# Down's ten full blocks in seven products for eight, on one Trainium2 core

## The reference

```python
def lora_add(base, inp, A, B):
    t = einsum('bri,bni->bnr', A[0][idx], inp)           # rank 16
    return base + einsum('bor,bnr->bno', B[0][idx], t) * 0.5
gate = lora_add(x @ W_gate.T, x, A_gate, B_gate)         # F = 2752
up   = lora_add(x @ W_up.T,   x, A_up,   B_up)
act  = silu(gate) * up
x1   = x + lora_add(act @ W_down.T, act, A_down, B_down) # the part called Down
base = x1 @ weight.T + bias                              # the part called out
out  = x1 + base + scale * ((x1 @ a_sel.T) @ b_sel.T)
```

## Time and profile before

| | us |
|---|---|
| median of three runs | 1662.97 |
| the profiled execution | 1659.71 |
| its span | 1657.6 |
| TensorE busy | 1620.2 |
| VectorE busy | 1138.4 |
| GpSimd busy | 653.5 |
| ScalarE busy | 500.8 |

### The profile page before, as it was taken

One profiled execution on the slowest core, in us unless ns is written; L12 is line 12 of the kernel. 1 busy time (PEld: TensorE's weight loads), 2 busy tenths in 40 slices (PEclk: granted clock), 3 DMA queues, 4 the chain that ended last, 5 costly groups with the idle time before them and its releaser, 6 DMA issues.

```text
span 1657.6 us, 20957 instructions
## 1 busy us (share of the span) xinstructions
PE 1620.2 (98%) x7060; PEld 1315.6 (79%) x7060; DVE 1138.4 (69%) x1302; ACT 500.8 (30%) x833; POOL 653.5 (39%) x441
## 2 busy tenths in 40 slices
PE   6989999999999899999999999999999999999998
PEld 4778888888887788888888788888888887778886
DVE  5987777777769877777777655666655578856433
ACT  3633333333346333333334221111111121431110
POOL 5244444444453444454444443233323331541110
PEclk9999999999999999999999999999999999999999
DMA  8334434433533345334334751122222131013322
GB/s 160 101 80 106 151 98 105 144 84 87 131 90 101 80 108 153 92 105 143 87 85 131 249 148 58 51 79 80 80 53 78 61 70 27 19 29 79 79 50 54
DMA packets 218125, 156.12 MB, mean 94 GB/s; under 512 B 110692, under 2 KB 200164, under 8 KB 215268
## 3 DMA queue, kind: packets, MB, share of 16 engines
q1 hardware_dynamic: 169536, 114.92, 27.4%
q10 hardware_dynamic: 48356, 39.86, 7.6%
q0 software_dynamic: 128, 0.00, 0.0%
HBM read 115.38 MB, written 39.32 MB: 93 GB/s over the span
## 4 chain that ended last, share of the span: by engine, by line
PE 64%; DVE 2%; POOL 1%; issue 1%; DMA 0%; ACT 0%; SPq 0%; DVEq 0%; ACTq 0%
PE ps L1958 64%; DVE tw_down L958 0%; POOL act L1884 0%; POOL Wd L1892 0%; DVE acc L950 0%; DVE X_T L608 0%; DMA raw<-in_x_dram 0%; POOL W L1843 0%; DVE Bd L904 0%; ACT W L1397 0%; DVE Bf L641 0%; DVE tw_down L933 0%; DVE tw_down L931 0%; DVE TU L508 0%; DVE ct L1077 0%
## 5 line engine op out<-in xcount | busy, mean ns | idle before, releaser
L1958 PE MATMUL ps<-X_T,W 128*128 128x512 f32 x1944 | 463.9, 393 | 13.0 <-DVE vbuf L688 5.1
L1958 PE MATMUL ps<-act,Wd 128*128 128x512 f32 x2016 | 462.2, 389 | 1.3 <-POOL Wd L1892 1.3
L1958 PEld LDWEIGHTS ps<-X_T,W 128*128 128x128 f32 x1944 | 365.9, 189 | 97.4 <-DVE vbuf L673 7.4
L1958 PEld LDWEIGHTS ps<-act,Wd 128*128 128x128 f32 x2016 | 378.4, 188 | 81.4 <-POOL Wd L1892 1.7
L1958 PE MATMUL ps<-X_B,W 128*128 128x512 f32 x1728 | 419.0, 392 | 15.3 <-ACT X_B L1426 12.8
L1958 PEld LDWEIGHTS ps<-X_B,W 128*128 128x128 f32 x1728 | 326.4, 189 | 86.6 <-issue 13.2
L950 DVE TENSOR_TENSOR acc<-acc,ps 128x1024 f32<-128x1024 f32 x176 | 214.1, 1219 | 176.5 <-PE ps L1958 175.8
L1843 POOL TENSOR_TENSOR W<-s,W 128x512 fp32r<-128x512 f32 x156 | 211.6, 1357 | 260.4 <-ACT W L1397 260.4
L1843 POOL TENSOR_TENSOR W<-TG,W 128x512 fp32r<-128x512 f32 x88 | 128.4, 1460 | 179.3 <-ACT W L1397 179.3
L1397 ACT ACTIVATE W<-s 128x512 fp32r<-128x512 f32 x156 | 98.4, 632 | 275.5 <-PE ps L1958 264.4
L1884 POOL TENSOR_TENSOR act<-stage,act 128x1024 fp32r<-128x1024 f32 x42 | 100.7, 2415 | 173.4 <-ACT act L1630 173.4
(11 more groups left out here) (135 smaller groups left out, 1522.7 us busy)
## 6 DMA issues: line engine op xcount, KB each, us to landing
stage<-act_scratch SPq DMA_DIRECT2D x21, 1024.0 KB, 5.0
raw<-in_L_cond_W_gate_dram SPq DMA_DIRECT2D x164, 128.0 KB, 3.0
raw<-in_L_cond_W_up_dram SPq DMA_DIRECT2D x164, 128.0 KB, 3.2
raw<-in_x_dram SPq DMA_DIRECT2D x104, 128.0 KB, 3.1
raw<-in_L_cond_W_down_dram SPq DMA_DIRECT2D x88, 128.0 KB, 3.3
act_scratch<-c21buf ACTq DMA_DIRECT2D x42, 256.0 KB, 2.4
act_scratch<-vbuf ACTq DMA_DIRECT2D x42, 256.0 KB, 2.8
xt_scratch<-xt ACTq DMA_DIRECT2D x4, 2048.0 KB, 6.6
```

The lines of the kernel that those rows point to most:

```text
L1958: return nc.tensor.matmul(dst, stationary, moving, start=start, stop=stop, skip_group_check=True)
```

## The change

Down's ten full blocks are now done in seven products for eight as well, over (two halves of the output tiles, even and odd) x (the two tiles of a block) x (two groups of 512 tokens). The work is cut into 140 steps:

- The ten blocks form two groups of five (`GROUP`). In a group the products come in the order P4, P2, P1, P5, P6, P3, P7, each for both halves `h` of the tokens: 28 stages (`B_STAGES`) of five steps. A step multiplies one block's stationary part (128 x 4 x 128) by one moving block (128 x 512): 4 banks x 3 = 12 matmuls. The five steps of a stage add up in the same four banks. In P2, P1, P3 and P7 two adapter matmuls follow each step.
- Seven banks are used in turn, four to a stage (`bank_of`), and the eighth holds the adapter's sums. When a stage has ended, VectorE adds each of its banks to one to four places of `acc` (`read_bank`) during the first three steps of the next stage.
- The moving blocks are act tiles (P1, P2, P3) or sums of them (P4 to P7). The sums T1 to T4 are made by VectorE in the gate/up stage, four subtractions for each pair of full units (`t_first`, `t_second` twice, `t_fourth`), and stored to HBM (`sums_scratch`). A second `vbuf` makes room for this.
- In Down each moving block is loaded by its own DMA of 256 KB into a ring of four (`load_moving`), its high part is made by ScalarE and its low part by GpSimd (`moving_low`), for both halves of the tokens. P7 needs a second moving block, B12, for the adapter; its low part is made by VectorE.
- The weights of eight blocks at a time are held unsplit in `DW` (`turn_down`). VectorE changes them in place into the sums (`down_sum`), and the parts for one product of five blocks are split into `Sr`.
- x is added to `acc` in 16 residual items, in the middle of Down, and no longer loaded into it.
- `turn_ad(bb)` for the blocks 1 to 10 runs at the steps of `AD_STEP`; SP loads for the step `q + 4`. The turns of `Bd`, `bd_low`, `td_first` and the copies they need now run after the last step.

The core of the diff:

```diff
+        PRODUCTS = ["P4", "P2", "P1", "P5", "P6", "P3", "P7"]
+        B_GIVES = {"P1": ("C11", "C12", "C21", "C22"), "P2": ("C11",), "P3": ("C12",), "P4": ("C21",),
+                   "P5": ("C12", "C22"), "P6": ("C12", "C21", "C22"), "P7": ("C21", "C22")}
+        B_STAGES = [(g, name, h) for g in range(2) for name in PRODUCTS for h in range(2)]
+        STEPS = GROUP * len(B_STAGES)
+        def raw_at_step(q):
+            items = []
+            if 40 <= q < 88 and q % 3 == 1:
+                items.append(("r", (q - 40) // 24, (q - 40) // 3 % 8))
+            if q in (-1, 0, 1):
+                items += [("D", q + 3, 0), ("D", q + 3, 1)]
+            if 22 <= q < 34 and q % 2 == 0:
+                items.append(("D", 5 + (q - 22) // 4, (q - 22) // 2 % 2))
+            if 61 <= q < 65:
+                items.append(("D", 8 + (q - 61) // 2, (q - 61) % 2))
...
+        AD_STEP = {1: 3, 2: 5, 3: 7, 4: 9, 5: 68, 6: 70, 7: 72, 8: 74, 9: 76, 10: 100}
...
+        def mv_step(n):
+            return MOVING[n - T_RING][0] + 1 if n >= T_RING else n - 3
+        def bank_of(s, p):
+            return (4 * s + p) % 7
...
+            def t_second(U):
+                n = pairs_before(U) + 1
...
+                V.tensor_tensor(vbuf0[:, :], vbuf1[:, :], vbuf0[:, :], ALU.subtract).then_inc(t_made[2], 1)
+                eng.wait_ge(t_stored[0], 16 * n)
+                V.tensor_tensor(t1buf[:, :], vbuf1[:, :], t1buf[:, :], ALU.subtract).then_inc(t_made[1], 1)
+
+            def t_fourth(U):
+                n = pairs_before(U) + 1
+                eng.wait_ge(act_stored[0], 16 * (U + 1))
+                eng.wait_ge(t_made[1], n)
+                V.tensor_tensor(c21buf[:, :], c21buf[:, :], t1buf[:, :], ALU.subtract).then_inc(t_made[3], 1)
...
@@ VectorE, unit(U)
                 if not plain(U - 1):
                     second_act(U - 1)
+                if u % 2:
+                    t_first(U - 1)
+                else:
+                    t_second(U - 1)
                 add_q(U)
...
                 if u in SPILL_UNITS:
                     turn_x(("y", h, SPILL_UNITS.index(u)))
+                if u % 2 == 0:
+                    t_fourth(U - 1)
                 add_v(U)
...
@@ VectorE, last_unit(U)
                 else:
-                    turn_item(("D", 0, 1))
+                    turn_down(0, 1)
                     half_tile_first(U)
                     turn_ad(0)
                 half_tile_second(U)
+                if h == 1:
+                    turn_down(1, 0)
+                    turn_down(1, 1)
...
@@ VectorE, Down
+            def turn_down(bb, e):
...
+                for c in range(2):
+                    last = V.transpose(
+                        DW[bb % len(DW)][:, c, :, e * 64:(e + 1) * 64].rearrange("p k (q i) -> p q k i", q=2),
+                        src[:, :].rearrange("p (q k c i) -> p c q k i", q=2, k=KT, c=2)[:, c])
+                last.then_inc(dw_turned.up((bb, e)), 1)
...
+            def read_bank(s, p):
+                eng.wait_ge(pe_s.sem, pe_s.after(("bank", s, p)))
+                for place in places_of(s, p):
+                    h, k, c = place
+                    dst, src = acc[h][:, k, c * TT:(c + 1) * TT], bank_b(bank_of(s, p))
...
+                        V.tensor_tensor(dst, dst, src, ALU.add).then_inc(acc_added.up((s, p, place)), 1)
...
+            def down_step(q):
+                s, banks = banks_at_step(q) if q >= 0 else (0, ())
+                for p in banks:
+                    read_bank(s, p)
+                    if p == 0 and s in T_STAGES:
+                        read_t_bank(s)
+                for item in raw_at_step(q):
+                    if item[0] == "r":
+                        add_residual(item)
+                for n in range(len(MOVING)):
+                    if mv_step(n) == q and mv_by_vector(n):
+                        moving_low(n)
...
+                    if at_ < len(STILL) and STILL[at_] in sw_sum.value:
+                        down_sum(STILL[at_])
+                for item in raw_at_step(q):
+                    if item[0] == "D" and item[1] < BLOCKS - 1:
+                        turn_down(*item[1:])
+                    elif item[0] != "r":
+                        turn_item(item)
+                for bb in range(1, BLOCKS):
+                    if AD_STEP[bb] == q:
+                        turn_ad(bb)
+                if q in (STEPS - 3, STEPS - 2):
+                    last_low(q - STEPS + 3)
...
-            for bb in range(BLOCKS - 1):
-                down_block(bb)
+            for q in range(-3, STEPS + 3):
+                down_step(q)
+            for pr in range(2):
+                td_first(pr)
+            for p in range(2):
+                bd_low(p)
+            for p in range(2, 4):
+                turn_item(("Bd", p))
             last_block()
...
@@ SP
+            def load_moving(n):
+                _, name, j, h = MOVING[n]
+                if n >= STAGING:
+                    wait_mv_low(sp, n - STAGING)
...
+            def down_step(q):
+                for n, moving in enumerate(MOVING):
+                    if moving[0] == q + 6:
+                        load_moving(n)
+                for item in raw_at_step(q + 4):
...
+                for bb in range(1, BLOCKS):
+                    if AD_STEP[bb] == q + 4:
+                        load_ad(bb)
...
@@ GpSimd
+            def down_step(q):
+                for n in range(len(MOVING)):
+                    if mv_step(n) == q and not mv_by_vector(n):
+                        moving_low(n)
+                for n in {-3: (0, 1), -1: (2,), 0: (3,), 1: (4,)}.get(q, ()):
+                    still_low(STILL[n])
+                if still_for(q - 1) is not None:
+                    still_low(still_for(q - 1))
...
@@ TensorE
+            def down_step(q):
+                s, j = divmod(q, GROUP)
...
+                eng.wait_ge(sw_lo, still_at[g, name, block_] + 1)
+                wait_mv_low(eng, n)
+                for p in range(4):
+                    if j == 0 and before_in_bank[s, p] is not None:
+                        wait_bank_read(eng, *before_in_bank[s, p])
...
+                    for wl, xl in THREE:
+                        last = matmul(bank_b(bank_of(s, p)), slot[:, wl, p, :], moving[:, xl, :],
+                                      start=(j == 0 and (wl, xl) == (0, 0)),
+                                      stop=(j == GROUP - 1 and (wl, xl) == (1, 0)))
```

756 lines of the change are left out of this document (474 added, 282 removed).

## The result

The changed kernel takes **1712.7 us** (median), the kernel before 1662.2 us: a ratio of 1.031, 95% interval 1.029 to 1.032. So it is slower, as forecast, but by some 50 us where 15 were forecast. The profiled execution has a span of 1710.5 us against 1657.6 us, 52.9 us more, and that is the sum to explain. Ratios leave out slow outliers, of which there was one, 3729 us in one of the twelve executions of e12_combined_start.

What follows compares the result with a forecast made beforehand. The prediction took TensorE, busy for 98% of the span, to bound the kernel. Its terms, -54.5 + 4.9 + 6.5 + 25 + 14 + 6 + 1 + 12 = +15 us, gave 1678 us (range 1664 to 1692).

Steps and rivals of the forecast that it cites:

- around the P7 stages: Down, around the two P7 stages: a loss of 1 us.
- What is removed: Down's ten blocks: 240 fewer matmuls at 0.227 us each save 54.5 us.
- Gate/up: New VectorE subtractions cost 4.9 us in eight even spill units and 6.5 us at the heads of the halves.
- The heads: Heads of gate/up's two halves: VectorE has no idle time, so the subtractions cost 6.5 us.
- Start of Down and the adapter chain: Down's first steps: serial adapter rounds of 9.5 us delay VectorE's bank read, holding TensorE at step 10; 25 us lost.
- The middle: Down, steps 68 to 76: the adapter turns of blocks 5 to 9 delay a bank read; 14 us (8 to 18).
- VectorE inside the stages: Down's stages where P1's reads, the sums for P6 and turns fall together on VectorE: 6 us (1 to 12).
- End of Down: After the last step: reads, adapter sums and B_down turns no longer lie under block 9; 12 us (9 to 15).
- Rival 1: Down: turns of adapter weights don't hold up bank reads, only start and end costs remain; 1649 us, chance 0.17.
- rival 2: Most is covered: gate/up takes the subtractions in idle time and sums don't collide; 1631 us, chance 0.06.
- Rival 3: New two-SBUF-operand VectorE operations wait for GpSimd and take 1.78 us each; 1697 to 1715 us, chance 0.17.

Runs made afterwards that it cites:

- e12_combined_start: Changed kernel with two adapter buffers, loads, turns and sums reordered, first adapter turn moved into step 2, first moving blocks loaded ahead of W_down pieces: 1666.2 us, 1.0027.
- e7: Changed kernel without the four activation sums per pair of gate/up units, their stores and waits; Down loads the activations' own blocks: 1697.6 us, 1.0218.
- e8: Changed kernel with the fourth sum moved on VectorE, in even units, behind the addition after P7: 1708.8 us, 1.0291.
- e5: Changed kernel with a second raw buffer for Down's adapter weights, steps of the turns unchanged: 1693.7 us, 1.0193.
- e2: Changed kernel with the residual additions taken out of steps 56 to 81 and the turns of blocks 8 and 9 two steps apart: 1703.2 us, 1.0248.
- e14: e12_combined_start with mid-Down weight loads two steps earlier, second moving block's high part earlier, last full block's parts later, B_down low parts moved: 1648.3 us, 0.9929.
- e3: Changed kernel with the last full block's 1 MB activation load put in block 6's place and issued one step earlier: 1705.1 us, 1.0272.
- e10: Kernel before the change with eight short TensorE pauses in Down, five small ScalarE copies each: 1678.9 us, 1.0114.
- e13: Kernel before the change with eight middle-length TensorE pauses in Down, ten small ScalarE copies each: 1704.3 us, 1.0259.
- e9: Kernel before the change with eight long TensorE pauses in Down, sixteen small ScalarE copies each: 1720.6 us, 1.0359.

## Why the prediction was wrong, step by step

The direction and most mechanisms were right; three terms failed. The forecast sum was +14.9 us and the measured one +52.9, so 38.0 are missing: 21.1 of half clock, which had no term; 12.5 around the P7 stages, where "1 us" stood and 13.5 were idle; 6.7 before step 135, which had no term. The other terms miss by -2.3 us in sum, since their errors cancel in part.

- *What is removed*, 54.5 us: 51.4 measured. A step is 2.74 or 3.21 us, not 2.73 or 3.18, and there are 140.
- *Gate/up*, 4.9 + 6.5: 16.5 us measured, all but 0.8 of it the sums with their stores and waits (e7). The 4.9 us stood in the units that were named, 0.6 us each (e8). The heads cost 9.5 us rather than 6.5, within their bounds and within what they scatter (6.1 to 11.0 us); the other units, put at nothing, cost 2.4 us in three places.
- *Start of Down and the adapter chain*, 25 us: right in mechanism (rounds of 9.3 to 9.7 us, the bank read behind turn_ad(4)) and near in size, 21.9 us idle where 1.3 was, with 11.2 at steps 8 to 10. e5 takes the round apart, and 4.1 us are left there.
- *The middle*, 14 us: 26 us idle. Step 75 waited, as forecast, but only 7.65 us of it is that step (12.5 with the two smaller waits ahead of it). The step that failed is "around the two P7 stages 1 us": VectorE's landings of blocks 8 and 9 and of the residual cost 7.4 us at step 65 and 6 more around it. With the loads moved apart 4.5 us stay at step 65 (e2), with the loads two steps earlier none (e14). I had priced VectorE's operations there and not asked when its operands land: W_down took 3.9 us to land, not 3.3, and six loads in four steps share three slots. The chain itself was right at 12.5 us for 14; that the forecast put it all into step 75 was not.
- *VectorE inside the stages*, 6 us: 0.7. The reads, sums and turns of the P1 stages fit. The reads took 676 ns and the sums 784 to 1171 ns, near the prices used. Where the margin came from no run shows; it may be that adding stage by stage counts what the engine spreads over the next one.
- *End of Down*, 12 us: 10.4 idle, and 12.7 us with what runs slower behind it. The idle part was near; that the total meets the forecast is in part luck, since half clock was not in it.
- Not in the sum at all: 6.7 us at step 135. ACT waits 6.6 us for the 1 MB load of the last full block, with the high parts of the moving blocks queued behind (e3). A wait was added on ACT, and the prediction did not name what stands behind it.
- Not in the sum at all, and the largest: **21 us of half clock**. TensorE ran without a break in the kernel before, so no row of Down showed what idle time costs behind it. A row of gate/up did: behind 2.58 us of waiting, twelve matmuls took 4.61 us instead of 2.9. I read the wait there and not the length beside it. The pauses put into the kernel before show the same without the change.

Idle time in Down was forecast at 55 to 60 us (the end's wait among it) and measured at 65.7; with the 1.7 us of the earlier trace rows for each of some ten waits the forecast would have stood near 1695 us. Rival 1 (chain covered) fell with e5, rival 2 with e7. Rival 3 (1697 to 1715 us) met the size by luck and not by its cause: the sums of two SBUF operands in gate/up took 0.67 to 0.85 us beside a busier GpSimd, not 1.78, and the product that took 1.78 now takes 1.34 us. The rule of the Trainium skill's "GPSIMD Engine Reference", section "Key points", on instructions with two SBUF inputs is not refuted by this. Of the 80 new subtractions only five took 1.6 to 1.8 us, while an old sum of two SBUF operands (s<-TG,s) took as long in five of 38 cases before and in 19 now. All these slow ones stood beside a GpSimd operation; how busy GpSimd is on the mean does not tell how many there will be.

## What to carry to other kernels

Price a wait of TensorE at its length plus what runs at half clock behind it, and look in the profile of before for a matmul group that is longer than its like behind a wait. When work is cut from the engine that bounds the kernel, list for each queue what lands and what is issued in the shorter stage, and not only what each engine computes: here loads, one single buffer and the order of two turns cost more than the products saved. The saving itself was real; with the loads and turns put in order and a second Ad_raw it showed as 14 us.

## What the runs showed of the hardware

- Behind idle pieces of 1.8, 3.5 and 5.5 us, TensorE's next 132 matmuls took 1.4 to 2.6 us longer in one, seven and eight of eight cases (e10, e13, e9). One piece of 1.76 us was enough. The slower stretch does not end with the first matmuls: in the changed kernel 12 matmuls at 1009.16 took 4.13 us for 2.90, although the wait ahead of them had ended 2.3 us earlier.
- Of 80 VectorE subtractions of two 128x512 operands in SBUF, 75 took 0.65 to 0.70 us and five 1.6 to 1.8. All five stood beside a GpSimd operation, but so did some of the others. A mean (0.67 to 0.85 us by line) hides this.
- Gate and up, unchanged between most of these kernels, ended at 944.5 to 949.3 us, so one profile per kernel can't tell differences of 3 us there. The scatter is in the heads of the halves (the period of unit 3 was 21.4 to 23.1 us in the first half and 21.4 to 24.6 in the second); from unit 4 to the end of a half a period repeated within 0.1 us.
